# Group-norm attention on one core: first image's queries without block products, GpSimd's residuals and row reduction behind the queries, last value tile ahead of the second shift

## What is computed

```python
xn = group_norm(x, gamma, beta)          # 32 groups, statistics over tokens and channels of a group
q = xf @ wq + bq;  k = xf @ wk + bk;  v = xf @ wv + bv
scores = einsum('bnc,bmc->bnm', q, k) * C ** -0.5
attn = softmax(scores, axis=-1)
out = einsum('bnm,bmc->bnc', attn, v) @ wp + bp
return out.reshape(B, H, W, C) + residual
```

## Time and profile before

| | us |
|---|---|
| three runs | 2183.1, 2192.78, 2194.34 |
| median | 2192.78 |
| profiled execution | 2178.84 |
| its span, first to last instruction | 2177.1 |
| TensorE busy in it | 2103.0 (97%), 9241 matmuls |
| VectorE busy | 1848.2 (85%) |
| GpSimd busy | 875.3 (40%) |
| ScalarE busy | 746.6 (34%) |
| mean granted TensorE clock | 0.993 of 2.4 GHz |

### The profile page before, as it was taken

One profiled execution on the slowest core, in us unless ns is written; L12 is line 12 of the kernel. 1 busy time (PEld: TensorE's weight loads), 2 busy tenths in 40 slices (PEclk: granted clock), 3 DMA queues, 4 the chain that ended last, 5 costly groups with the idle time before them and its releaser, 6 DMA issues.

```text
span 2177.1 us, 28352 instructions
## 1 busy us (share of the span) xinstructions
PE 2103.0 (97%) x9241; PEld 1730.8 (80%) x9241; DVE 1848.2 (85%) x2564; ACT 746.6 (34%) x1221; POOL 875.3 (40%) x482
## 2 busy tenths in 40 slices
PE   6989999999999999999999999999999999999999
PEld 5767777788787887878787787887778878787887
DVE  7888897898988989888897988889789898888864
ACT  3332332423325233332423325233242334324232
POOL 4345343343425334353343435334253334434433
PEclk8999999999999999999999999999999999999999
DMA  6203012030120302012030120302103030120201
GB/s 169 59 1 116 1 43 74 0 116 0 48 67 10 106 0 85 31 34 82 5 111 0 48 67 10 106 0 77 38 14 101 0 103 12 42 74 10 68 1 59
DMA packets 110268, 108.13 MB, mean 50 GB/s; under 512 B 8476, under 2 KB 74016, under 8 KB 110240
## 3 DMA queue, kind: packets, MB, share of 16 engines
q1 hardware_dynamic: 107984, 103.58, 15.6%
q10 hardware_dynamic: 2256, 4.20, 0.7%
HBM read 74.19 MB, written 33.55 MB: 49 GB/s over the span
## 4 chain that ended last, share of the span: by engine, by line
PE 60%; issue 17%; DVE 12%; POOL 6%; ACT 3%; DMA 1%; POOLq 0%; DVEq 0%; ACTq 0%
PE psum L1200 9%; PE psum L1201 9%; PE psum L1202 9%; PE psum L1175 5%; PE psum L1177 5%; PE psum L1176 5%; PE psum L1101 4%; PE psum L1104 4%; PE psum L1103 4%; POOL total_part L431 3%; POOL total_part L440 2%; DVE score L851 2%; DVE bn L697 2%; PE psum L1029 2%; PE psum L1031 2%
## 5 line engine op out<-in xcount | busy, mean ns | idle before, releaser
L1200 PE MATMUL psum<-v_hi,pt_hi 128*128 128x512 f32 x1024 | 401.0, 392 | 26.7 <-DVE v_lo L680 25.0
L1201 PE MATMUL psum<-v_lo,pt_hi 128*128 128x512 f32 x1024 | 399.0, 390 | 0.0
L1202 PE MATMUL psum<-v_hi,pt_lo 128*128 128x512 f32 x1024 | 399.0, 390 | 0.0
L408 POOL TENSOR_TENSOR x_res<-x_res,out_bias 128x512 f32<-128x512 f32 x128 | 203.1, 1610 | 336.3 <-DMA x_res<-in_x_dram 214.9
L680 DVE TENSOR_TENSOR pt_lo<-score,pt_hi 128x512 fp32r<-128x512 f32 x256 | 294.2, 1179 | 27.0 <-POOL total_part L431 25.3
L431 POOL TENSOR_TENSOR total_part<-total_part,score 128x512 f32<-128x512 f32 x192 | 308.7, 1608 | 16.6
L587 ACT ACTIVATE score<-psum 128x512 f32<-128x512 f32 x256 | 152.5, 596 | 368.8 <-PE psum L1177 368.8
L1200 PEld LDWEIGHTS psum<-v_hi,pt_hi 128*128 128x128 f32 x1024 | 192.6, 188 | 73.3 <-DVE v_lo L680 28.4
L1202 PEld LDWEIGHTS psum<-v_hi,pt_lo 128*128 128x128 f32 x1024 | 192.5, 188 | 40.3
L1201 PEld LDWEIGHTS psum<-v_lo,pt_hi 128*128 128x128 f32 x1024 | 192.7, 188 | 39.3
L1175 PE MATMUL psum<-pt_hi,xn_hi 128*128 128x512 f32 x512 | 200.9, 392 | 12.0 <-DVE pt_hi L680 12.0
(11 more groups left out here) (150 smaller groups left out, 4038.6 us busy)
## 6 DMA issues: line engine op xcount, KB each, us to landing
x_res<-in_x_dram SPq DMA_DIRECT2D x128, 256.0 KB, 3.0
out_dram<-x_res SPq DMA_DIRECT2D x128, 256.0 KB, 2.3
x_blk<-in_x_dram SPq DMA_DIRECT2D x240, 128.0 KB, 3.2
score<-in_x_dram SPq DMA_DIRECT2D x16, 128.0 KB, 8.1
w_q<-in_L_conv_wq_dram SPq DMA_DIRECT2D x1, 1024.0 KB, 5.6
w_k<-in_L_conv_wk_dram SPq DMA_DIRECT2D x1, 1024.0 KB, 8.3
w_v<-in_L_conv_wv_dram ACTq DMA_DIRECT2D x1, 1024.0 KB, 9.4
w_p<-in_L_conv_wp_dram ACTq DMA_DIRECT2D x1, 1024.0 KB, 13.0
```

The source lines that it names most:

```text
L408: last = nc.gpsimd.tensor_tensor(at, at, out_bias[:, first:end], ALU.add)
L1200: nc.tensor.matmul(dst, hi[:, m, queries], v_hi[:, m, :], start=m == 0, stop=False)
L1201: nc.tensor.matmul(dst, hi[:, m, queries], v_lo[:, m, :], start=False, stop=False)
L1202: end = nc.tensor.matmul(dst, lo[:, m, queries], v_hi[:, m, :], start=False, stop=m == NT - 1)
```

## The change

1. **First image's queries are plain.** `first_queries(h)` multiplies all 4 x 4 blocks of `A` for one half of the tokens: 4 chunks x 4 x 3 = 48 matmuls a half. The order on TensorE is now half 0, value tiles 0 and 1, half 1. Chunk j uses bank (2 + j) mod 4. No sums of xn are made for image 0; a fourth plain block, A21, gets parts of its own. Block products begin with image 1, and their semaphores count from there (`earlier`).
2. **Block residuals move from GpSimd to VectorE**: four plain blocks ahead of `group_variance(0)`, four sums behind the first `norm`. ScalarE makes the high parts of the plain blocks ahead of its eight DMA issues for `w_k` and `w_q`. `root(0)` comes behind all four block sums.
3. **GpSimd**: the bias chain starts after the first half's queries; from image 1 on the four residuals and the row's all-reduce wait for the image's last block product.
4. **VectorE**: in image 0 the five `sum_products` and the row stand between the value parts and the second half's residuals; in `queries` the low part of t[0], chunk 3, comes ahead of a sum; `variance` ahead of the last two `pt_lo`; the last value part ahead of `tile_shift(b, 1)`.
5. **SyncE** loads image 1 once `w_q` is there and the blocks are made. `a_full` and some scratch lie elsewhere.

```diff
-                sp.wait_ge(s_prod, PRODUCTS)
+                sp.wait_ge(s_again[1], 16 * NI)
+                sp.wait_ge(s_set, SET_WV + KC)
+                sp.wait_ge(s_as, len(SUMS))
+                sp.wait_ge(s_abl, len(WHOLE))
...
-            def block_lo(at, whole):
-                pool.wait_ge(s_abh, at + 1)
-                nc.gpsimd.tensor_tensor(ab_lo[:, at], whole, ab_hi[:, at].bitcast(FP32),
-                                        ALU.subtract).then_inc(s_abl, 1)
...
             block_sum(S3, a11, a21, ALU.subtract)
-            root(0)
             pool.wait_ge(s_as, 2)
             block_sum(S2, ab_sum[:, S1], a11, ALU.subtract)
             pool.wait_ge(s_as, 3)
             block_sum(S4, a12, ab_sum[:, S2], ALU.subtract)
-            for at, whole in ((A11, a11), (A12, a12), (A22, a22)):
-                block_lo(at, whole)
-            for at in (S1, S2, S3, S4):
-                block_lo(at, ab_sum[:, at])
-            pool.wait_ge(s_prod, PRODUCTS)
+            root(0)
+            pool.wait_ge(s_first, KC)
...
                     pool.wait_ge(s_bias, BIAS_STEPS)
                 else:
+                    pool.wait_ge(s_prod, b * PRODUCTS)
                     for i in range(TH):
...
+            def first_query_hi(h, j):
+                act.wait_ge(s_first, h * KC + j + 1)
+                nc.scalar.activation(t_hi[h][:, j, :], first_bank(j), ACT.Identity, bias=wk_bq[:, j:j + 1]).then_inc(s_th, 1)
...
+            act.wait_ge(s_seth, SET_A_LAST + 1)
+            for at, c, r in WHOLE:
+                nc.scalar.activation(block_parts(at)[0], whole_block(c, r), ACT.Copy).then_inc(s_abh, 1)
...
+                if starts(b):
+                    act.wait_ge(s_setv, SETV_WK_BQ)
+                    for j in range(KC):
+                        first_query_hi(0, j)
+                        if j == 0:
+                            second_split()
                 v_hi_part(b, 0)
                 v_hi_part(b, 1)
-                queries(b)
+                if starts(b):
+                    for j in range(KC):
+                        first_query_hi(1, j)
+                else:
+                    queries(b)
                 for m in range(NT):
...
+            def first_query_lo(h, j):
+                dve.wait_ge(s_th, h * KC + j + 1)
+                nc.vector.scalar_tensor_tensor(out=t_lo[h][:, j, :], in0=first_bank(j), scalar=wk_bq[:, j:j + 1],
+                                               in1=t_hi[h][:, j, :].bitcast(FP32), op0=ALU.add,
+                                               op1=ALU.subtract).then_inc(s_tl, 1)
+            def block_lo(at, made, whole):
+                dve.wait_ge(s_abh, made)
+                hi, lo = block_parts(at)
+                lo_part(lo, whole, hi, s_abl)
             def queries(n):
...
+                    if p:
+                        dve.wait_ge(s_th, n * 8 + 4 * p + 3)
+                        lo_part(t_lo[0][:, 2 + p, :], t_sum[0][:, 2 + p, :], t_hi[0][:, 2 + p, :], s_tl)
...
                                                    op0=ALU.add, op1=ALU.add).then_inc(s_tc, 1)
-                    dve.wait_ge(s_th, n * 8 + 4 * p + 3)
-                    lo_part(t_lo[0][:, 2 + p, :], t_sum[0][:, 2 + p, :], t_hi[0][:, 2 + p, :], s_tl)
+                    if not p:
+                        dve.wait_ge(s_th, n * 8 + 4 * p + 3)
+                        lo_part(t_lo[0][:, 2 + p, :], t_sum[0][:, 2 + p, :], t_hi[0][:, 2 + p, :], s_tl)
...
+            for n, (at, c, r) in enumerate(WHOLE):
+                block_lo(at, n + 1, whole_block(c, r))
...
-            for k in range(KC):
-                first_norm(k, 1, s_norm)
-            dve.wait_ge(s_norm, KC)
-            block_sums(0)
-            def first_row():
+            def first_queries():
+                first_query_lo(0, 0)
+                for k in range(KC):
+                    first_norm(k, 1, s_norm)
+                first_query_lo(0, 1)
+                second_lo_parts()
+                first_query_lo(0, 2)
+                first_query_lo(0, 3)
+                v_lo_part(0, 0)
+                v_lo_part(0, 1)
                 dve.wait_ge(s_again[1], 16 * NI)
                 sum_products(KC, 2 * KC + 1)
                 dve.wait_ge(s_setv, SETV_VECTORS - 1)
                 nc.vector.tensor_scalar(bqbk_part[:], bqbk[:], 1.0 / P, None, ALU.mult).then_inc(s_setv, 1)
                 dve.wait_ge(s_setv, SETV_VECTORS)
-                for k in range(KC):
-                    row_part(0, k)
+                for j in range(KC):
+                    first_query_lo(1, j)
+                    row_part(0, j)
             def image(b, more):
-                v_lo_part(b, 0)
-                v_lo_part(b, 1)
-                queries(b)
                 if starts(b):
-                    first_row()
+                    first_queries()
+                else:
+                    v_lo_part(b, 0)
+                    v_lo_part(b, 1)
+                    queries(b)
                 for m in range(NT):
                     if more and m == NT - 1:
                         dve.wait_ge(s_sv, (b + 1) * STAT_STEPS + 1)
...
                         group_variance(b + 1)
                     if m > 1:
                         pt_lo_parts(b, 0, m - 2, m - 1)
-                pt_lo_parts(b, 0, NT - 2, NT)
                 if more:
                     variance(b + 1)
+                pt_lo_parts(b, 0, NT - 2, NT)
                 for m in range(2, NT - 1):
                     v_lo_part(b, m)
                     if more and m == 4:
                         norm(b + 1)
+                    if starts(b) and m == 4:
+                        for n, at in enumerate(SUMS):
+                            block_lo(at, len(WHOLE) + n + 1, ab_sum[:, at])
                 totals(b, 0)
+                v_lo_part(b, NT - 1)
                 tile_shift(b, 1)
-                shifts(b, 1, 0, TH)
-                v_lo_part(b, NT - 1)
-                shifts(b, 1, TH, NT)
+                shifts(b, 1, 0, NT)
...
+                elif what in (("v", 0, 0), ("v", 0, 1)) and starts(n):
+                    pe.wait_ge(s_tl, 3 + what[2])
...
+            def first_queries(h):
+                tokens = slice(h * BANK, (h + 1) * BANK)
+                for j in range(KC):
+                    if h and j < 2:
+                        pe.wait_ge(s_tl, j + 1)
+                    elif h:
+                        pe.wait_ge(s_free, j - 1)
+                    elif j == 1:
+                        pe.wait_ge(s_setr, lo_rank(SET_M) + 2)
+                    elif j == 0:
+                        pe.wait_ge(s_setr, lo_rank(SET_M) + 1)
+                    for k in range(KC):
+                        at, c, r = WHOLE[2 * (j // 2) + k // 2]
+                        if h == 0 and j % 2 == 0 and k % 2 == 0:
+                            pe.wait_ge(s_abl, 2 * (j // 2) + k // 2 + 1)
+                        if j == 0:
+                            if h:
+                                pe.wait_ge(s_xl, k + 1)
+                            else:
+                                pe.wait_ge(s_xl0, k + 1)
+                        hi, lo = (part[:, k % 2, chunk(j % 2)] for part in block_parts(at))
+                        nc.tensor.matmul(first_bank(j), hi, xn_hi[:, k, tokens], start=k == 0, stop=False)
+                        nc.tensor.matmul(first_bank(j), hi, xn_lo[:, k, tokens], start=False, stop=False)
+                        last = nc.tensor.matmul(first_bank(j), lo, xn_hi[:, k, tokens], start=False, stop=k == KC - 1)
+                    last.then_inc(s_first, 1)
...
+                if starts(b):
+                    first_queries(0)
                 v_tile(b, 0)
                 v_tile(b, 1)
-                queries(b)
+                if starts(b):
+                    first_queries(1)
+                else:
+                    queries(b)
```

More of the change, by code:

```diff
@@ L147, in group_norm_attention @@
         out_bias = sb("out_bias", [P, C])
+        with ExitStack() as setup:
+            a21_hi, a21_lo = (sb(n, [P, 2, C // 2], F32R, where=setup) for n in ("a21_hi", "a21_lo"))
         shift = sb("shift", [P, BANK])
@@ L297, in group_norm_attention, with whole_block, block_parts, first_bank @@
         SUM_AT = ((1, 1), (0, 1), (0, 0), (1, 0))
-        def sums_of(n):
-            return first_sums if starts(n) else x_t
-        def sums_lo_of(n):
-            return first_sums_lo if starts(n) else xs_lo
+        WHOLE = ((A11, 0, 0), (A12, 1, 0), (A21, 0, 1), (A22, 1, 1))
+        SUMS = (S1, S2, S3, S4)
+        def whole_block(c, r):
+            return a_full[:, 2 * c:2 * c + 2, r * C // 2:(r + 1) * C // 2]
+        def block_parts(at):
+            return (a21_hi[:], a21_lo[:]) if at == A21 else (ab_hi[:, at], ab_lo[:, at])
+        def first_bank(j):
+            return work[(2 + j) % 4]
+        def earlier(n):
+            return n - 1
         EXPS = {0: (0, 2), 1: (2, 4), 2: (4, 6), 3: (6, NT)}
@@ L784, in queries @@
+            def block_lo(at, made, whole):
```

(10 more changed lines are left out.)

147 lines of the change are left out of this document (60 added, 87 removed).

## The result

The changed kernel takes 2139.68 us in the median of 4 runs (2138.01 to 2139.97), against 2192.11 (2183.1 to 2194.34) for the kernel before: a ratio of 0.9767 [0.9739, 0.9795]. The forecast was 2125, within 2112 to 2150: the time lies in the range, 14.7 us above the point. Its profiled execution took 2139.97 us, so what is missing can be read from the two traces.

The account below looks back on a forecast made before the run. TensorE, busy 97% of the span, was taken as the bound, gains coming from its waits, clock or matmul count. First image -16.5 and steady part -37.6 give -54.1 us from the profiled 2178.84: 2124.7, say 2125, range 2112 to 2150.

Parts of the forecast that it names:

- The first image: Image 0: start -5.3, queries -2.9, statistics -8.3, out tiles 0; total -16.5 us.
- bank wait: First image's queries: first value tile waits for bank 0 until VectorE has made the third chunk's residual; about 0.9 us.
- The queries were right: Images 1 to 15: four query waits, 12.0 us, removed with restarts and a lower-clock stretch, about 15.5 us.
- The race: Row reduction at Q (score start) + 12.0, third maximum at Q + 11.8 slips through; if held, 2143 us, chance 0.22.
- rival 3: Beside the scores the reduction holds VectorE its whole 6.13 us instead of 5.1: +12, 2137 us; chance 0.06.
- The value wait: Images 1 to 14: TensorE's wait for the last value tile's low half goes, with restarts, -24.6 us.
- +1.5 us: Images 1 to 14: later waits for the second half's pt_lo, with 0.15 us of room if the chain comes 0.8 earlier.
- 1 for jitter: Steady part: 1 us added for jitter, beside the residuals and row reduction placed next to the scores.
- the forecast's own case: Whole kernel: -16.5 in the first image and -37.6 in the steady part, about 2125 us; chance 0.54.
- more than 1 us per image in a new TensorE wait: TensorE: a sign that the forecast is wrong; pt_lo waits were expected under 0.5 us.
- rival 2: Images 1 to 14: value wait becomes a pt_lo wait, variance not moving the chain: 2132 us; chance 0.10.
- The 14 us between profiled and timed: Kernel before: timed median above profiled execution, explained by three or four more collisions of about 3.9 us, which vanish too.

Follow-up runs that it names:

- the last experiment: The changed kernel with the query residual of chunk 3 behind the sum again: 2151.7 us, ratio 0.9832 against the kernel before.
- The variance experiment: The changed kernel with variance behind the last two pt_lo again: 2143.13 us, ratio 0.9789 against the kernel before.
- variance at m = 6: The changed kernel with variance moved earlier, after the maximum and pt_lo of m = 6: 2132.21 us, ratio 0.9776 against the kernel before.
- the row alone waits: The changed kernel with GpSimd's residuals run at once and only the row reduction waiting for the last block product: 2136.1 us, ratio 0.9763.
- both together: The changed kernel with only the row reduction waiting and variance after m = 6 as well: 2142.87 us, ratio 0.978 against the kernel before.
- value part 7 back: The changed kernel with the last value part behind four shifts of the second half again: 2155.57 us, ratio 0.9848 against the kernel before.

## Why the prediction was right and where it failed

**The first image was right.** -7.3 and -8.4 us against -8.2 and -8.3, the first query at 46.51 against 46.5, one out tile wait of 3.1 us against about 3. The queries gave 2.0 us where the sum has 2.9: their 120 matmuls take 30.7 us, at a granted clock of 0.91 over the stretch, so 3.0 us besides the bank wait are lost where 1.6 were left in. Two details differ: a wait of 3.0 us for `dev` in the setup, behind the four new block residuals, which the forecast had as "about 2.5 us hidden" without a wait; and a bank wait of 0.44 in place of 0.9.

**The queries were right.** No query wait is left (17.6 us with small change, against 15.5), and the fourth maximum is held in all 14 images, with `dev` in time. The race was as close as said: moving one subtraction turns it (the last experiment). In the rows above the held maximum waits out part of a 6.28 us reduction and ends 5.2 us after that one's start (1658.17 - 1652.95). In the earlier trace rows it was 5.1 of 6.13. The end is the steady side: in all 14 images the held maximum ends 1.05 us before the reduction does. So rival 3 fell. By the Trainium skill (SBUF — State Buffer, Who interferes with whom) the holder keeps the pair for its whole instruction, which the page says of a VectorE instruction in a 2-port mode; the trace disagrees in length here too, and again in the last experiment (held to 1141.62, 5.07 us after the reduction's start).

**The value wait was removed as said** (the experiment that brings it back costs 16 us), and the forecast even named what is late next. **The step that failed is the "+1.5 us" for it:** "if it comes 0.8 us earlier, 0.15 us of room stay". TensorE comes to the seventh low half 1.74 us earlier, as forecast (Q + 88.07 in the earlier trace rows, Q + 86.33 now, the wait taken off). Two of its inputs were wrong.

- The room. It was read from one image: there the last pair starts at Q + 86.24. The median over the images of the same trace is Q + 86.67, so the room was 0.7 us, not 1.1.
- The chain. The last pair was to come 0.8 us earlier; it comes 0.05 later (Q + 86.72).

Together 0.7 - 1.74 - 0.05 = -1.1: images 1 to 14 hold 15.7 us of this wait, where the forecast had 1.5, and 1 for jitter. What a wait costs beyond itself can be read too. Without the value wait of 1.59 us TensorE comes 1.74 us earlier, so a restart is 0.15, as forecast. But the new wait has a restart as well: an image of before without a collision, less its wait, is 128.63 us long, and 12 of the 14 of after, less theirs, are 128.61 to 128.67. So the new wait costs 15.7 us, 2.1 of restarts and 0.8 of small change in images 8 and 11, 18.6 us in all, 16.1 more than forecast. The value wait gave 24.4 (14 x 1.74) against 24.6. That makes the 16.4 by which all else in images 1 to 14 is short (-5.7 against -22.1). The collisions gave 2.1 more than forecast, the first two stages 0.8 less and the rest 0.3 less, which makes the 15.3 between the profiled executions (2139.97 against 2124.7).

So the time lies in the range, but the forecast's own case is not what happened. One of its signs of being wrong came true: "more than 1 us per image in a new TensorE wait"; it is 1.12. This is rival 2, which had a chance of 0.10, at a higher price: that gave 2132 for a chain that doesn't move, but with 1.1 us of room. (The chances of the cases, 0.54 and those of the rivals, add up to 1.02.)

**Why the chain did not move.** The variance does come earlier: `g_var` is at Q + 48.99 in the median, at Q + 49.54 before. (1) It would be 1.2 earlier, but the held maximum ends the seventh 0.59 later (forecast 0.4). (2) The root now runs beside a `pt_lo` and takes 2.04 us in place of 1.06; before, it ran beside a `v_lo` that reads PSUM. The variance experiment shows this by itself. So the total's reduction starts at Q + 57.20, even 0.36 later than before. (3) That costs only 0.16 at its end, since before it was held at its start: it takes 3.64 us where it takes 3.25 clear of `norm`, which ends at Q + 57.17. In the four kernels in which it starts between Q + 56.66 and 56.84, it ends at Q + 60.28 or 60.29 in each. (4) Value part 7 now stands ahead of the shift operation and delays it by 0.6 us more; the shifts behind it get this back, and end at Q + 69.35 against 69.20. Had the chain come 0.8 us earlier as forecast, it would have met `norm`; the kernels in which it does show that `norm` then pays (5.40 and 6.12 us) and value part 6 is late for the first out tile; what is left is still a gain, 0.6 us per image with the variance at m = 6.

The Trainium skill has the rule for (2) and (3): in SBUF — State Buffer, Who interferes with whom, it says that an instruction with one SBUF input outside the 2-port modes doesn't contend with GpSimd, while a `tensor_scalar` can enter such a mode and then does. The rows agree: the root takes 1.06 us beside the `v_lo` that reads PSUM, two `bn` statistics take 1.28 us at Q + 12.4 beside the row reduction, and `norm` grows from 2.98 to 6.12 us beside the total's. The forecast looked for such pairs only where a new all-reduce was placed, not where the moved root and the old one would meet `pt_lo` and `norm`.

**The 14 us between profiled and timed** before the change vanished, as said: after, the profiled 2139.97 and the median 2139.68 are one. Runs of before scatter over 2174 to 2204, those of kernels without query collisions over 1.5 to 6. A collision costs 2.8 to 6.9 us of image time (133.06 and 137.07 against 130.22), so four more of them would do it. That more of them lie in the slower executions is argued from this and not counted, since each kernel has one trace.

**Open.** How the last pair follows from the shifts' end. Over the kernels, 0.66 us at the shifts gave 0.74 at the last pair (variance at m = 6), and 0.16 at the shifts gave 0.45 when the row alone waits; between them lie exponentials, `xn_lo`, and GpSimd's totals that share time with each `pt_lo` (3.5 us for two in place of 1.28). Nor was the hold of `norm` and the reduction on each other measured by itself; it rests on the ends that don't move and on the kernels in which the two overlap.

## What to carry to other kernels

A gap that closes on one engine moves the whole demand behind it forward: the room of what is late next must be read over all images, not one, and the move of its chain has to be carried through every step that another engine can hold, since an operation that starts earlier behind a fixed obstacle ends at the same time. When two engines exclude each other, every move ahead of them is a race; ask which pairs will meet in the new order, also among instructions that the change doesn't touch. And a wait that trades random collisions for a small constant cost can leave the median where it is and still be worth having for even times.

## What the runs showed of the hardware

- The gap of about 5.8 us between GpSimd's tensor operation and an all-reduce begins behind a semaphore wait that stands between them: with the residuals over 4.3 us before Q, the reduction started at Q + 6.5, 6.3 us after the last block product had ended (both together, Q = 734.61).
- `norm` (TENSOR_SCALAR, SBUF to SBUF) and a partition all-reduce hold each other off: 2.98 us alone, 5.40 to 6.27 beside it; the total's reduction takes 3.46 to 3.99 in place of 3.25, and the top reduction behind it 2.26 to 2.73 in place of 1.88 (variance at m = 6, and both together).
- A VectorE subtraction or maximum with both inputs in SBUF that the row reduction holds ends 1.05 us before the reduction does, in every image of the traces of before and after where there is such a hold (5.08 to 5.51 us after the start of a reduction of 6.13 to 6.57 us).
- A root on 128 x 4 elements takes 1.06 us beside a `v_lo` that reads PSUM, 1.44 at m = 6, and 2.04 beside a `pt_lo` with both inputs in SBUF.
- The value wait of TensorE cost its own length and 0.15 us of restart: without its 1.59 us TensorE came 1.74 us earlier (Q + 88.07 and Q + 86.33).
- In the experiment with value part 7 back, images with a TensorE wait of 1.6 to 1.7 us show no stretch at the lower clock behind it; of nine waits of 1.8 to 2.4 us, four were followed by a stretch at the lower clock (0.51 over 2 us), which cost 1.6 to 1.8 us more.
